# A causal mask moved from TensorE into VectorE's row-maximum pass, in the second attention of a fused transformer block

## What is computed

```python
q = rmsnorm(q, q_norm_w).transpose(0, 2, 1, 3)
k = rmsnorm(k, k_norm_w).transpose(0, 2, 1, 3)
q = apply_rope(q, cos, sin); k = apply_rope(k, cos, sin)
k = jnp.repeat(k, n_rep, axis=1); v = jnp.repeat(v, n_rep, axis=1)
scores = jnp.einsum('bhqd,bhkd->bhqk', q, k) * scale
causal = jnp.tril(jnp.ones((S, S), bool))
scores = jnp.where(causal[None, None], scores, jnp.finfo(scores.dtype).min)
attn = jnp.einsum('bhqk,bhkd->bhqd', jax.nn.softmax(scores, axis=-1), v)
hidden = hidden + attn @ o_w.T
```

## Time and profile before

| | |
|---|---|
| time, median of three runs | 1299.55 us (1298.91 to 1302.46) |
| span of the profiled execution | 1300.3 us |
| TensorE busy | 1241.6 us, 95% |
| TensorE weight loads | 1110.2 us, 85% |
| VectorE busy | 805.6 us, 62% |
| ScalarE busy | 653.8 us, 50% |
| GpSimd busy | 422.3 us, 32% |
| the second attention's steps, first maximum to last exps | about 670 to 1088 us |

### The profile page before, as it was taken

How to read it: one execution, slowest core, us unless ns; L and a number is a source line. 1 busy time by engine, 2 the same in 40 slices (tenths; PEclk the granted TensorE clock), 3 DMA queues, 4 the chain that set the end, 5 groups by cost and what they waited for, 6 DMA issues and landing times. The chain is left out here.

```text
span 1300.3 us, 23464 instructions
## 1 busy us (share of the span) xinstructions
PE 1241.6 (95%) x8088; PEld 1110.2 (85%) x8120; DVE 805.6 (62%) x1569; ACT 653.8 (50%) x1780; POOL 422.3 (32%) x499
## 2 busy tenths in 40 slices
PE   6999999999999999899979999999999998999998
PEld 5888999989998999788868888888898886788887
DVE  3666454335433543476668888888878876865554
ACT  3455444444444444545547676676667665333232
POOL 4111311131113111423376666666666660000000
PEclk9999999999999999999989999999999998999999
DMA  9100000000000020220110000000000021413210
GB/s 338 42 1 2 17 1 17 1 2 1 17 1 2 1 82 1 97 98 16 33 45 2 2 1 2 2 1 0 0 0 0 0 89 53 114 56 98 97 51 21
DMA packets 25166, 45.58 MB, mean 35 GB/s; under 512 B 3008, under 2 KB 15680, under 8 KB 24064
## 3 DMA queue, kind: packets, MB, share of 16 engines
q1 hardware_dynamic: 25024, 44.44, 10.1%
q10 hardware_dynamic: 64, 0.07, 0.0%
HBM read 42.30 MB, written 2.20 MB: 34 GB/s over the span
## 5 line engine op out<-in xcount | busy, mean ns | idle before, releaser
L493 POOL TENSOR_TENSOR p<-p,rinv 128x512 f32<-128x512 f32 x64 | 66.7, 1041 | 415.8 <-DVE rinv L1032 415.6
L762 ACT ACTIVATE p<-bank,nb,rq 128x128 f32<-128x128 f32 x256 | 113.8, 454 | 115.0 <-DVE nb L1240 115.0
L620 ACT ACTIVATE p<-bank,nmax 128x128 f32<-128x128 f32 x256 | 90.5, 366 | 119.6 <-DVE nmax L1020 119.6
L546 POOL TENSOR_TENSOR qr<-qr,rb 128x512 f32<-128x512 f32 x64 | 81.9, 1280 | 102.5 <-DVE rb L1206 102.1
L1429 PE MATMUL bank<-cur_hi,wqk_hi 128*128 128x512 f32 x256 | 110.1, 430 | 3.5 <-DVE cur_lo L973 3.5
L1028 DVE COPY pt<-bank 128x512 f32<-128x512 f32 x64 | 44.2, 690 | 110.6 <-PE bank L1447 107.8
L1429 PE MATMUL bank<-cur_hi,wqk_lo 128*128 128x512 f32 x256 | 102.9, 402 | 0.0
L1429 PE MATMUL bank<-cur_lo,wqk_hi 128*128 128x512 f32 x256 | 102.6, 401 | 0.0
L629 ACT ACTIVATE o_hi<-bank,bqkv 128x512 fp32r<-128x512 f32 x64 | 44.1, 688 | 101.1 <-PE bank L1457 101.1
L1036 DVE SCALAR_TENSOR_TENSOR o_lo<-bank,bqkv,o_hi 128x512 fp32r<-128x512 f32 x64 | 48.0, 750 | 51.8 <-ACT o_hi L629 51.8
L1688 PE MATMUL bank<-wo_hi,o_hi 128*128 128x256 f32 x256 | 74.4, 291 | 4.1 <-DVE o_lo L1279 4.1
(11 more groups left out here) (210 smaller groups left out, 4048.1 us busy)
## 6 DMA issues: line engine op xcount, KB each, us to landing
wqk_raw<-in_wqk SPq DMA_DIRECT2D x8, 512.0 KB, 9.9
gate<-gates_scratch SPq DMA_DIRECT2D x8, 512.0 KB, 3.7
cw<-combination_scratch SPq DMA_DIRECT2D x16, 256.0 KB, 3.2
xres<-in_x SPq DMA_DIRECT2D x4, 512.0 KB, 9.3
wv_raw<-in_wv SPq DMA_DIRECT2D x8, 256.0 KB, 9.9
wo_raw<-in_wo SPq DMA_DIRECT2D x8, 256.0 KB, 10.0
w_raw<-in_w SPq DMA_DIRECT2D x2, 1024.0 KB, 5.8
wq_raw<-in_wq SPq DMA_DIRECT2D x1, 2048.0 KB, 9.4
```

What stands on the lines that cost most here:

```text
L493: nc.gpsimd.tensor_tensor(p1[:, h % 2], p1[:, h % 2], rinv[:, h % 2].unsqueeze(2).broadcast_to([P, GB, T]), ALU.mult).then_inc(a_pn, 1)
L546: nc.gpsimd.tensor_tensor(qr[:, s.u % 2], qr[:, s.u % 2], rb[:], ALU.add).then_inc(g_qr, 1)
L620: last = nc.scalar.activation(p1[:, h % 2, b], bank[3][:, b * T:(b + 1) * T], ACT.Exp, bias=nmax[:, h % 2, b:b + 1], accum_out=rsum[:, h % ...
L762: last = nc.scalar.activation(p2[:, (s.u - 3) % 2, j], bank[3][:, j * T:(j + 1) * T], ACT.Exp, scale=rq[:, (s.u - 3) % 4, j:j + 1], bias=n ...
```

## The change

The mask is no product on TensorE any more. The four score products each write their 128 columns of bank 3 alone. VectorE's row maximum over 512 columns becomes four passes, one for each head: each reads 128 columns of bank 3 and `mask_f`, adds them, writes the sum to a new SBUF tile `sm`, and keeps the maximum. The exps read `sm` and not the bank. The maximum has no turned sign now, so `rq` is negated beforehand in two small operations to `nrq`. Bank 3 is free for the next scores when the four passes are done (`g_mx`), where it was after the exps (`g_ex`). `sm` has two slots, guarded by `g_ex` of the head two before. The bf16 mask and identity with their set-up copies fall away.

```diff
@@ tiles
-        mask = sb("mask", [P, REP * T], BF16, at=W2 + 45 * KB)
-        ident_b = sb("ident_b", [P, P], BF16, at=W2 + 46 * KB)
+        sm = sb("sm", [P, 2, REP, T], at=W + 22 * KB)
+        nrq = sb("nrq", [P, REP], at=W + 26 * KB)
@@ ScalarE, step
-                        last = nc.scalar.activation(p2[:, (s.u - 3) % 2, j], bank[3][:, j * T:(j + 1) * T], ACT.Exp,
+                        last = nc.scalar.activation(p2[:, (s.u - 3) % 2, j], sm[:, (s.u - 3) % 2, j], ACT.Exp,
@@ VectorE, set-up in the layer before
-                            nc.vector.tensor_copy(mask[:].rearrange("p (j s) -> p j s", j=REP),
-                                                  mask_f[:].unsqueeze(1).broadcast_to([P, REP, T])).then_inc(g_tab, 1)
-                            nc.vector.tensor_copy(ident_b[:], ident[:]).then_inc(g_tab, 1)
@@ VectorE, step
+                    if s.had(5):
+                        dve.wait_ge(g_ex, n - 4)
+                    dve.wait_ge(g_rq, n - 2)
+                    nc.vector.tensor_scalar(nrq[:, 0:REP // 2], rq[:, (s.u - 3) % 4, 0:REP // 2], -1.0, None, ALU.mult)
                     dve.wait_ge(g_sp, n - 2)
-                    nc.vector.tensor_reduce(nmax[:, (s.u - 3) % 2], bank[3][:].rearrange("p (j s) -> p j s", j=REP), X,
-                                            ALU.max, negate=True).then_inc(g_mx, 1)
-                    dve.wait_ge(g_rq, n - 2)
+                    nc.vector.tensor_scalar(nrq[:, REP // 2:REP], rq[:, (s.u - 3) % 4, REP // 2:REP], -1.0, None, ALU.mult)
+                    for j in range(REP):
+                        last = nc.vector.tensor_tensor_reduce(
+                            out=sm[:, (s.u - 3) % 2, j], in0=bank[3][:, j * T:(j + 1) * T], in1=mask_f[:], scale=1.0,
+                            scalar=-3.0e38, op0=ALU.add, op1=ALU.max, accum_out=nmax[:, (s.u - 3) % 2, j:j + 1])
+                    last.then_inc(g_mx, 1)
                     dve.wait_ge(g_mx, n - 2)
-                    nc.vector.tensor_tensor(nb[:, (s.u - 3) % 2], nmax[:, (s.u - 3) % 2], rq[:, (s.u - 3) % 4],
+                    nc.vector.tensor_tensor(nb[:, (s.u - 3) % 2], nmax[:, (s.u - 3) % 2], nrq[:],
                                             ALU.mult).then_inc(g_nb, 1)
@@ TensorE, step
                     if s.had(3):
-                        pe.wait_ge(g_ex, n - 2)
-
-                    pe.matmul(bank[3][:], ident_b[:], mask[:], start=True, stop=False, skip_group_check=True)
+                        pe.wait_ge(g_mx, n - 2)
                     for j in range(REP):
                         js = slice(j * T, (j + 1) * T)
                         last = pe.matmul(bank[3][:, js], q_t[:, s.u % 2, js], k_t[:, slot, kv * T:(kv + 1) * T],
-                                         start=False, stop=(j == REP - 1), skip_group_check=True)
+                                         start=True, stop=True)
                     last.then_inc(g_sp, 1)
```

More of the change, by code:

```diff
@@ L1194, in _ @@
                 ffn1(g, False)
-            dve.wait_ge(g_tab, 6)
+            dve.wait_ge(g_tab, 4)
             def rotate(out_cos, out_sin, src, table, cos_free, sin_free, done):
```

## The result

The changed kernel takes **1314.89 us** (median of 4 runs, 1311.85 to 1318.74) beside 1301.01 us for the kernel before (4 runs, 1298.91 to 1302.59). The ratio is 1.0109, with a 95% interval of 1.0087 to 1.0132, so the change costs 14 us. The forecast was 1332 us (1311 to 1366). Slower was right, and the time is inside the range, but the loss is less than half of the one forecast. The profiled executions agree: 1312.9 against 1300.3 us.

The account below looks back on a forecast made before the run. The prediction took a closed VectorE-ScalarE ring as the bound: +0.77 us over 64 steps is 49.3 us, less 16.7 of room, +32.6. From 1300.3 that gives 1332.9, less 0.75 profiling offset, 1332 us; range 1311 to 1366.

Parts of the forecast that it names:

- The closed ring: Second attention: VectorE and ScalarE wait only for each other, 5.44 us per plain step, and the edit adds work there.
- The mask product: TensorE before the scores: 64 products of 0.21 us removed, 13.4 us, a gain entirely lost in waits.
- Bank 3 free earlier: Scores wait for g_mx, not g_ex; VectorE's maximum never stood idle for scores, so nothing is gained.
- The pass on VectorE: Between pt_lo and nb: negations, four passes and accumulator reads take 1.52 us against 0.79, +0.73 on every step.
- its low end: Bound with free reads and passes of 0.18: 1.11 us from pt_lo to nb, 1306 us in all.
- Exps from SBUF: ScalarE's four exps read SBUF instead of PSUM: 0.01 us each, +0.04 per step.
- The room: What the ring waits for from outside between 665 and 1092 us: 16.7 us, 0.26 per step over 64 steps.
- The negations: Rival: VectorE's negations wait for GpSimd's rq, 0.43 us in 64 steps, 27.5 us more, 1360 us; chance 0.05.
- The clock rival: TensorE's granted clock falls in the loop as its busy share drops: +34 us, 1366 us; chance 0.03.
- The draw: Rival: reads nearly free and pt_lo to nb partly off the ring, 1300 to 1303 us; chance 0.04.
- the gained product: Rival: TensorE stays the bound, so the mask product's 13.4 us come off, 1286 us; chance 0.06.
- the two terms on the ring: VectorE's pass, +0.73 us, and the exps from SBUF, +0.04: together +0.77 us per step, 49.3 us over 64 steps.

Follow-up runs that it names:

- e7: Changed kernel with VectorE's pt_lo moved behind the next step's nb in every step: 1324.43 us, ratio 1.0183.
- e8: Kernel before the change, with VectorE's pt_lo moved behind the next step's nb: 1310.82 us, ratio 1.0081.
- e9: Changed kernel with pt_lo moved behind the next step's nb, except in each sequence's first step and the group's turn: 1310.31 us, ratio 1.0074.
- e10: e9 with VectorE's three looped passes written out and rq negated by one instruction, not two: 1299.49 us, ratio 0.9991.
- e11: e10 with masked scores written back into bank 3, exps reading them there, and TensorE waiting for the exps: 1305.58 us, ratio 1.0035.
- e1: Changed kernel with the mask product put back on TensorE before the scores, VectorE's mask passes kept: 1315.14 us, ratio 1.0096.
- e4: Changed kernel with TensorE waiting for the exps again and the exps reading bank 3, without the mask: 1315.78 us, ratio 1.0097.
- the unrolled kernel: Changed kernel with VectorE's three looped passes of the second attention written out, so VectorE never jumps back: 1308.71 us, ratio 1.0058.

## Why the prediction was right in direction and off in size

- **What bounds the kernel: right.** The closed ring of VectorE and ScalarE sets the plain steps. The product put back costs nothing, 0.60 us more work gives 0.60 us more per plain step, and pt_lo off the ring makes the step shorter. That the ring sets every step was not right.
- **The mask product, 13.4 us "entirely lost in waits": right for the changed kernel** (1315.14 against 1314.89 us).
- **Bank 3 free earlier, nothing: right** to what the times can tell (1315.73 us with the old wait); 0.2 to 0.5 us a pass in the trace.
- **The pass on VectorE, +0.73 us: the term that failed.** It measured +0.31 (1.10 against 0.79). The pass itself was well sized, 0.21 us to the next start against 0.20. The reads were put at 0.09 each and cost none between passes; the negations take 0.07 each, not 0.09; from the last pass's start it is 0.33 us to nb, where I had 0.20 + 0.16 + 0.11. The prediction had 0 for the read among its bounds (its low end, 1.11 us from pt_lo to nb, is right to 0.01) and chose 0.09, "since the read stands in the queue like any small operation". That choice was the error: of the 0.42 us too much, three pairs of pass and read make 3 x (0.29 - 0.21) = 0.24, the end 0.14 and the negations 0.04.
- **Exps from SBUF, +0.04: wrong, +0.17.** The earlier trace rows compare copies of 512 columns into another type, with no accumulator and one constant scale; the exps are 128 columns and start every 0.435 us from a bank, every 0.48 from SBUF. The estimate from the Trainium skill that the prediction set aside (Perfetto Trace Analysis, Optimizing Scalar/DVE Operations), 0.17 us a step, is what the trace shows.
- **The room, 16.7 us: right** (15 us, 12 to 18). Its place was not: it lies in the first steps of the sequences, not 0.26 in each.
- **Missing: the jumps back.** Two waits of 2.8 and 2.5 us for code, 6.2 us by the kernel that has none. I had counted what the added instructions take to run, and not what they do to the length of the loop.
- **The rivals.** The negations were not held by GpSimd: they start at 913.95 and 914.02, right behind pt_lo, 0.74 us into the 1.02 of GpSimd's rq, and take 0.16 us each. Beside another GpSimd operation they are held, as e7 to e11 show. The clock rival didn't come true in this kernel either: the granted clock stayed at 1.00 in the loop, with TensorE busy for 96% of it. But e1, e4, e7 and e8 did fall to the lower level inside the loop, after waits of TensorE of 1.8 to 4.1 us at a group's start; in the changed kernel waits of 1.64 and 1.92 us at that place went by without it. The timeline of GpSimd and the window of the changed kernel's second pass show both. The draw and the gained product fell with the result.

```profile
913.21 1.02 POOL L562 TENSOR_TENSOR rq<-q_ve,neg_half 128x4 f32<-128x4 f32 x1
```

```profile
868.00:977.00 109.00, 104.20 (x672) 89.62 (x672) 91.17 (x314) 71.85 (x208) 67.04 (x80) 1.00 0.00 0
```

The sum, made again. The plain step grew by 0.44 us (0.31 + 0.17, less 0.05 by which pt_lo starts sooner behind pt_hi, 0.62 against 0.67 us): 64 x 0.44 = 28 us; less the room of 15 = 13; with the jumps, 6, that is 19 us, where 14 were measured. The 5 us that are left over are about what the product is worth in the steps that TensorE sets (5.4 us in the kernel before), and the unrolled kernel fits that: 28 - 15 - 5 = 8, measured 7.4. But the product put back into the changed kernel cost 0.25 us, with an interval of some 5 us either way, and nothing in its passes once the step at the lower clock is set aside. The old wait for bank 3, put back by itself, cost 1.2 us in the three passes together. It may be that either of the two suffices to give TensorE that room and that only both together take it away, or that the room is larger for 0.44 us a step than it was for 0.60. No run puts both back into the changed kernel, so the 5 us stay open.

Of 32.6 us forecast, then, the two terms on the ring took away 64 x (0.77 - 0.44) = 21 us, the jumps put 6 back, and some 5 are the open rest. That the time fell inside the stated range is in part luck: the block from pt_lo to nb alone was put too high by 64 x 0.42 = 27 us, which would have given 1305 us, under the range. The exps (64 x 0.13 = 8 us) and the jumps (6 us), both too low in the forecast, made up for half of it.

## What to carry to other kernels

Follow the engines round before trusting a busy share: a product taken from an engine that is 95% busy was worth 5 us of 13 in one kernel and nothing that could be measured in the other, because two half-busy engines waited for each other. Follow them again after each edit: once pt_lo was off the first loop, a second one closed at 5.2 us, with an operation of GpSimd in its way. When an edit adds instructions to a loop, count the length of the body as well as their time, and look ahead of the first instruction behind each jump for idle time that is put down to nothing. Where the trace has no row for an operation, take its price from a row of the same width and form, and let a run with one more of it (here the second maximum) measure the room before the change is judged. And before a longer pass is put down to the edit, look at the granted clock in it.

## What the runs showed of the hardware

- A read of VectorE's accumulator (DVE_READ_ACCUMULATOR2_ANT, 82 ns) overlaps the next pass in full. The pass that adds, keeps and reduces 128 columns takes 284 ns, and the next starts 0.21 us later. With its output in PSUM the pass takes 318 ns, the read 138, and the next pass starts 0.25 us later.
- The same exp of 128 x 128 took 455 ns from PSUM and 480 to 484 from SBUF, and its start to start 0.435 and 0.48 us, while copies of 512 columns showed no difference (616 and 620 ns).
- A jump back over 416 to 418 instructions of VectorE stood for 2.4 to 2.8 us, with 36 or 37 packets on the queue of instructions; over 274 it did not stand, with 25.
- A negation of VectorE, one source on SBUF and 2 or 4 columns wide, ran beside GpSimd's rq (128 x 4, 1.02 us) without waiting, 0.16 us, wherever in rq it started. Beside GpSimd's multiplication of 128 x 512 (1.04 us) the same negation was held until that ended: 0.40 us, up to 0.54.
- After waits of 1.77 and 1.93 us TensorE's granted clock fell to 0.50 for some 3 us (e1, e4), and its products of 512 columns started every 0.43 us in place of 0.23: 1.5 us on the step. After waits of 1.92 and 1.64 us at the same place of the changed kernel it stayed at 1.00, so the length of that one wait doesn't decide it.
